# Moving the last shared products and the second half's slot table into the first steps of a loop over sorted expert tiles

## The reference

```python
E = 8; TOP_K = 2; D = 256; DE = 176; DS = 352
shared = jax.nn.silu(x @ Ws_gate) * (x @ Ws_up) @ Ws_down
scores = jax.nn.softmax(x @ W_router, axis=-1)
topk_vals, topk_idx = jax.lax.top_k(scores, TOP_K)
onehot = jax.nn.one_hot(topk_idx, E, dtype=x.dtype)
combine = jnp.einsum('bsk,bske->bse', topk_vals, onehot)
...
h = jax.nn.silu(jnp.einsum('td,edh->eth', xf, We_gate)) * jnp.einsum('td,edh->eth', xf, We_up)
y_all = jnp.einsum('eth,ehd->etd', h, We_down)
routed = jnp.einsum('etd,te->td', y_all, combine)
return routed.reshape(b, s, d) + shared
```

## Time and profile before

| | us |
|---|---|
| median of 3 runs | 673.24 |
| lowest and highest | 670.88, 677.87 |
| the profiled execution | 682.33 |
| its span | 680.6 |

### The profile page before, as it was taken

The page is one execution under the profiler, slowest core; times in us unless marked ns, Lnnn a source line. Parts: engine busy times, 40 slices in busy tenths (PEclk is TensorE's granted clock), DMA queues, the critical chain, the costliest instruction groups (busy, mean ns, idle before and its releaser), DMA issues. The chain is left out here.

```text
span 680.6 us, 16745 instructions
## 1 busy us (share of the span) xinstructions
PE 604.4 (89%) x5027; PEld 460.5 (68%) x5027; DVE 490.6 (72%) x991; ACT 403.7 (59%) x829; POOL 320.1 (47%) x442
## 2 busy tenths in 40 slices
PE   3688877999999968899999999999896799989995
PEld 2577766788888866555555555554674698988874
DVE  2878886688887877889989989983675444444755
ACT  3888883344434431789889889989542154544331
POOL 2455555133232557746656666552675044034163
PEclk9999997999999977799999999999799699999997
DMA  5434448300000024444434444430013145455243
GB/s 162 117 99 133 117 119 298 125 1 1 0 0 1 23 71 141 122 117 152 135 116 145 136 119 143 137 106 6 1 40 110 52 155 171 126 163 172 84 148 116
DMA packets 72601, 71.20 MB, mean 105 GB/s; under 512 B 12364, under 2 KB 68812, under 8 KB 72556
## 3 DMA queue, kind: packets, MB, share of 16 engines
q1 hardware_dynamic: 67324, 56.33, 27.7%
q0 software_dynamic: 5232, 14.29, 6.7%
HBM read 38.48 MB, written 31.36 MB: 103 GB/s over the span
## 5 line engine op out<-in xcount | busy, mean ns | idle before, releaser
L1441 DVE TENSOR_REDUCE a_smax<-a_s 128x2 f32<-128x512 f32 x256 | 165.3, 682 | 16.5 <-PE a_s L1363 11.4
L1259 ACT ACTIVATE a_prob<-a_st 128x512 f32<-128x512 f32 x256 | 141.9, 597 | 20.8 <-PE a_st L1353 19.8
L1353 PEld LDWEIGHTS a_st<-qop,kop 64*128 64x128 f32 x512 | 71.6, 189 | 60.1 <-DVE a_smax L1441 27.9
L1363 PE MATMUL a_s<-kop,qop 64*128 64x256 f32 x512 | 108.8, 323 | 0.0
L1353 PE MATMUL a_st<-qop,kop 64*128 64x256 f32 x512 | 105.2, 317 | 3.4 <-DVE a_smax L1441 2.6
L1315 PE MATMUL last_banks<-a_prob,a_vt 128*32 128x256 f32 x1024 | 82.0, 393 | 3.2 <-ACT a_pv_sb L1244 1.5
L832 POOL TENSOR_TENSOR f_hs_lo<-f_kept,f_hs_hi 128x512 fp32r<-128x512 f32 x32 | 41.3, 1321 | 85.3 <-ACT f_hs_hi L782 85.3
L1363 PEld LDWEIGHTS a_s<-kop,qop 64*128 64x128 f32 x512 | 75.1, 196 | 0.0
L1892 POOL DMA_INDIRECT sorted_rows<-m_xn,m_slot x32 | 32.4, 1014 | 45.0 <-PE m_gu L128 27.4
L126 PE MATMUL f_bank<-f_xt_hi,w_hi 128*128 128x512 f32 x128 | 51.1, 399 | 1.2 <-DVE w_raw L878 0.6
L128 PE MATMUL f_bank<-f_xt_hi,w_lo 128*128 128x512 f32 x128 | 50.3, 393 | 0.0
(11 more groups left out here) (296 smaller groups left out, 1682.3 us busy)
## 6 DMA issues: line engine op xcount, KB each, us to landing
qop<-qop_rows SPq DMA_DIRECT2D x64, 100.0 KB
kop<-kop_rows SPq DMA_DIRECT2D x64, 96.0 KB
sorted_rows<-x_all SPq DMA_DIRECT2D x2, 2944.0 KB, 15.4
qop<-sorted_rows SPq DMA_DIRECT2D x46, 128.0 KB
expert_rows<-turned SPq DMA_DIRECT2D x46, 128.0 KB
kop_rows<-k_hi SPq DMA_DIRECT2D x32, 128.0 KB
qop_rows<-q_hi POOLq DMA_DIRECT2D x30, 128.0 KB, 2.7
x_all<-in_x SPq DMA_DIRECT2D x4, 512.0 KB, 3.8
```

Source lines behind the costliest of these rows:

```text
L1259: act.activation(prob[:, u % 8], st_ps[BANK[u]][:], ACT.Exp, scale=SCALE1).then_inc(prob_ready, 1)
L1353: st = pe.matmul(st_ps[BANK[u]][:, c * D:(c + 1) * D], lhsT=kop[t.slot][rows, u // 2, c * P:(c + 1) * P], rhs=qop[t.slot][rows, u // 2], s ...
L1363: sm = pe.matmul(s_ps[BANK[u]][:, c * D:(c + 1) * D], lhsT=qop[v.slot][rows, w // 2, c * P:(c + 1) * P], rhs=kop[v.slot][rows, w // 2], st ...
L1441: dve.tensor_reduce(smax[:, v.slot, opposite(u)], s_ps[BANK[u]][:].rearrange("p (q n) -> p q n", q=2), AX_X, ALU.max).then_inc(smax_ready, 1)
```

## The change

Four moves, and two waits that follow them. `shared_down(4)` leaves its place ahead of the loop and stands in step 0, behind `turn(0)`; `shared_down(5)` stands in step 2, behind `turn(2)`. `slots(1)` is cut in two: its first seven steps, now `placed(1)`, stay where they were, the rest with `table(1)` goes into step 0 of VectorE's loop, behind the low part of pair 0. `residual(1)` and the scaling of `mix` go into its step 2, behind the low part of pair 2. The expert numbers of the first half now wait for the first 12 table steps only and those from pair 11 on for all 24; `hidden(1)` waits for 19 steps, where it waited for the slots of both halves.

```diff
--- before.py
+++ after.py
@@ -1552,6 +1552,7 @@
         N = GROUPS * SHC
         CHAIN = 17
         TABLE = 12
+        PLACED = 7
         LOGITS = TILES * E
         PLACES = (PT + 1) * E
         LAST_FIRST = (PART_TILES - 1) // 2
@@ -1614,7 +1615,7 @@
                 else:
                     pe.wait_ge(plain_ready, (g - 1) * DC)
                 if g == 2:
-                    pe.wait_ge(table_steps, 7)
+                    pe.wait_ge(table_steps, PLACED)
                 route(pe, misc, second.plain if g == 1 else plain, wr, g).then_inc(logit_done, 1)
 
             def places(b):
@@ -1682,13 +1683,12 @@
                     router(3)
                 if n == 4:
                     places(1)
-            shared_down(HEAD - 2)
-            shared_down(HEAD - 1)
-
             expert_of = {}
 
             def load_experts(p):
                 if p == 0:
+                    pe.wait_ge(table_steps, TABLE)
+                if p == LAST_FIRST:
                     pe.wait_ge(table_steps, TABLE * PARTS)
                 for j in range(2):
                     expert_of[2 * p + j] = pe.value_load(experts_t[0:1, 2 * p + j:2 * p + j + 1], min_val=0, max_val=E - 1)
@@ -1713,7 +1713,7 @@
                     pe.wait_ge(silu_ready, HEAD)
                 else:
                     pe.wait_ge(hid_ready, HEAD)
-                    pe.wait_ge(slot_ready, PARTS)
+                    pe.wait_ge(table_steps, TABLE + PLACED)
                 for j in range(2):
                     e = expert_of[2 * p + j]
                     for dc in range(DC):
@@ -1761,6 +1761,10 @@
                     hidden(s - 2)
                 if s < PAIRS1:
                     turn(s)
+                if s == 0:
+                    shared_down(HEAD - 2)
+                if s == 2:
+                    shared_down(HEAD - 1)
                 if s == PAIRS1 + 2:
                     shared_hidden(HEAD)
                 if s >= 3:
@@ -1992,8 +1996,7 @@
                 op.then_inc(table_steps, 1)
                 dve.wait_ge(table_steps, b * TABLE + k)
 
-            def slots(b):
-                sl = tiles_in(b)
+            def placed(b):
                 counted = misc[:, place_cols(b)]
                 dve.wait_ge(place_done, b + 1)
                 if b == 0:
@@ -2007,6 +2010,9 @@
                 entry(b, 6, dve.tensor_tensor(begins[:], ends[:], tiles_of[:], ALU.subtract))
                 entry(b, 7, dve.scalar_tensor_tensor(place[:], over_tiles(begins[:]), float(P),
                                                      counted[:, 0:PT * E].rearrange("p (t e) -> p t e", e=E), ALU.mult, ALU.add))
+
+            def slots(b):
+                sl = tiles_in(b)
                 for k in range(TOP):
                     op = dve.tensor_tensor(picked[:, k], chosen[:, k, sl], place[:], ALU.mult)
                 entry(b, 8, op)
@@ -2030,6 +2036,7 @@
             choices(0)
             turned_low(1)
             multiply(0)
+            placed(0)
             slots(0)
             table(0)
             for n in range(1, HEAD):
@@ -2044,12 +2051,8 @@
                 if n == 4:
                     residual(0)
                 if n == 5:
-                    slots(1)
-                    table(1)
+                    placed(1)
             hidden_low(HEAD - 1)
-            residual(1)
-            dve.tensor_tensor(mix[:].rearrange("p k t -> p (k t)"), mix[:].rearrange("p k t -> p (k t)"),
-                              gates[:, 3:4].to_broadcast([P, TOP * TILES]), ALU.mult).then_inc(mix_ready, 1)
 
             dve.wait_ge(h_clear, 1)
             for s in range(PAIRS1 + 3):
@@ -2070,6 +2073,13 @@
                     dve.wait_ge(xthi_ready, s + 1)
                     dve.tensor_tensor(xt[1][:, s % 2], xt_ps[:].rearrange("p (c n) -> p c n", c=2),
                                       raw(xt[0][:, s % 2]), ALU.subtract).then_inc(xt_ready, 1)
+                if s == 0:
+                    slots(1)
+                    table(1)
+                if s == 2:
+                    residual(1)
+                    dve.tensor_tensor(mix[:].rearrange("p k t -> p (k t)"), mix[:].rearrange("p k t -> p (k t)"),
+                                      gates[:, 3:4].to_broadcast([P, TOP * TILES]), ALU.mult).then_inc(mix_ready, 1)
                 if s == PAIRS1 - 1:
                     dve.wait_ge(mix_ready, 1)
                     dve.wait_ge(shared_added, PT)
```

## The result

| | before | after |
|---|---|---|
| median, us | 676.38 | 673.76 |
| lowest and highest | 670.88, 684.63 | 667.17, 677.23 |
| runs | 20 | 20 |
| the profiled execution | 682.33 | 667.17 |
| its span | 680.6 | 665.4 |

The ratio of after to before is 0.9942, 95% interval 0.9921 to 0.9963: 0.6% faster, some 3.9 us of 676.4. Forecast were 668.2 us in the range of 664.0 to 673.5; the median of 673.76 lies 0.26 us above that range.

A forecast was written before the change was run, and what follows sets the result against it. TensorE bounds the loop, so the gain is how much earlier its first `turn_hidden` comes: 5.0 us with the clock falling in both kernels. 673.24 - 5.0 = 668.2 us, range 664.0 to 673.5.

The forecast's parts named there:

- The base: Whole kernel: the median of 673.24 us, from which the 5.0 us gain was subtracted to give 668.2.
- the 5.0 of the sum: Way into the loop: first `turn_hidden` 5.0 us earlier, with the clock falling to half in both kernels.
- What the change wins is therefore how much earlier the join comes: Whole kernel: gain equals how much earlier the join (first `turn_hidden`, 544.63 us before) comes, plus what the clock does.
- The steps on VectorE and TensorE: Way into the loop: reordered work leaves the path, so hidden(0) begins at 532.9 instead of 539.47, 6.6 us earlier.
- The idle 0.8 us forecast ahead of turn(1): TensorE ahead of turn(1): one idle time of about 0.8 us, where 2.35 and 1.76 stood.
- The clock: TensorE ahead of the loop: half clock until about 538.7 in the new kernel, covering hidden(0), turn(2) and most of down(5).
- rival 1: Way into the loop: clock stays up in the new kernel only, 7.9 us and 0.3 more, 665.0 us; chance 0.25.
- Rival 2: Ahead of the loop: turn(0) waits for its data, down(4) behind it; gain 0 to 2 us, 672.2; chance 0.20.
- the sign that I named as proof against the prediction: TensorE at turn(0): an idle time ended by a load would show the prediction wrong.
- Rival 3: Way into the loop: late pair 0 data decides turn(1) in both kernels; costs 0.6 to 2.6 us, to 675.8; chance 0.10.
- Rival 4: First three loop steps: residual(1) ahead of `m_gxt_lo` loses 1.66 us in each, giving the gain back, 673; chance 0.05.
- the slack of 1.1 us: First loop step: `m_gxt_lo`, 1.9 us behind the first `turn_hidden`, is ahead of down(0)'s need at 3 us.

The follow-up runs named there:

- after_half_c: The kernel after with only each token's first choice scattered in the first half, on a chip without stretches: 660.48 us, ratio 0.9858 to the kernel before.
- again: The kernel after, unchanged, run once more on a chip without stretches: 666.86 us, ratio 0.9986 to the kernel before.
- before_look: The kernel before, unchanged, run once for its trace on a chip without stretches: 665.56 us.
- before_half_b: The kernel before with only each token's first choice scattered in the first half, on a chip with stretches: 672.24 us, ratio 0.9900 to the kernel before.
- after_half: The kernel after with only each token's first choice scattered in the first half, on a chip with stretches: 669.65 us (4 runs), ratio 0.9830 to the kernel before.

## Why the prediction was wrong, point by point

**The base.** The step that put the time out of the range is "I carry the difference over: 673.24 - 5.0 = 668.2". That median of three runs was 3.1 us below the median of twenty, 676.38, with the runs from 670.9 to 684.6. With the same 5.0 us and the base of 676.38 the time would have been 671.4. As a ratio the forecast was 668.2 / 673.24 = 0.9925, against 0.9942 (0.9921 to 0.9963) in the first comparison and 0.9926 on the other chip with stretches. The class, under 1% faster, held. A forecast given as a ratio would have held too: 0.9925 lies in the interval. That the gain of 3.9 us lies so near the 5.0 of the sum is in part luck. The join moved by 2.5 us more than I had, and over 3 us of it did not reach the time. So a second step failed, though it did not decide the range: "What the change wins is therefore how much earlier the join comes". The next step took 0.2 us of it back (0.7 where the old kernel has full clock in it), and some 3 us more are unexplained.

**The steps on VectorE and TensorE** held in the trace of the first comparison. Turn(0) begins at the end of down(3) with no wait for a load (523.73); hidden(0) follows turn(1) by 1.49 us, where I had 1.75; down(5) fills the wait for `m_h`; slots and table cost nothing beside turn(1). The idle 0.8 us forecast ahead of turn(1) is absent, since down(4) filled it at half clock. Down(3)'s start to hidden(0) was to take 6.07 us (526.83 to 532.9) and took 6.41.

**The clock** was mis-sized. I took the half clock for hidden(0), turn(2) and down(5), 6.7 us from hidden(0) to the join; it took 3.88, at full clock. It fell ahead of that, during down(3), turn(0) and down(4), where it costs little, since at full clock turn(1) waits for the low part of pair 0 instead: down(3) to turn(1) took 4.92 us, and 4.70 in after_half_c at full clock, with 1.31 of them idle. I had 4.32. (The rule that I drew from the Trainium skill, "TensorE: Matmul & The Clock Gate", section "A second HAM failure mode: psum-queue depth-cycling", had the fall stay in both kernels. It stayed in after and is absent from 519 to 528 in after_half_c.) The term at the join was 5.0 and measured 7.5, nearer to rival 1 (7.9), and yet rival 1's time did not come: 7.5 at the join gave 3.9 in the time.

**Rival 2** was the missing condition. In the one trace taken in the first comparison it did not occur, so its 0.20 is not shown wrong there; the mistake was to treat it as chance within one chip. I worked it out from the three stretches of the earlier trace rows for a "median run" of the same chip. It goes with the chip, or with the time at which it was used, which can't be told apart here since each was used once: three of them show no such stretch in any trace, run the kernel before in 666.6 to 668.9 us, and give the change 0.1 to 0.3%. In again down(3) ends near 521.6, turn(0) stands until 527.20, and against before_look the join moves by 1.0 to 1.2 us; I had 522, 527 and 0.3 (0 to 2). There the sign that I named as proof against the prediction, a turn(0) whose idle time is ended by a load, stands in the trace. The 20 runs of the first comparison look like those of a chip with stretches: both profiled traces have them, and the runs spread as widely as on the other (672.7 to 686.2).

**Rival 3** did not occur; where landings are traced, pair 0 lands 2.6 us behind its load, not with the last of the eight. **Rival 4**, as a loss of 1.66 us in each of three steps, did not either, but a loss of 0.7 us in one step did, and it comes from the slack of 1.1 us that I had behind `m_gxt_lo`. I set its start, 1.9 us behind the join, against down(0) at 3 us. It started at 1.95 us, but it takes 0.68 us, and the last transpose of turn(3) began 2.7 us behind the join. Down(0) followed the end of `m_gxt_lo` by 0.14 us: the slack was gone.

## What to carry to other kernels

Work moved out of a wait pays only if the wait's other end does not have its own date: write down when the data lands beside when the engine would be ready, and treat their order as the condition of the whole sum. Here that order differed from chip to chip, so one trace gave the right mechanism and a gain that three of the five later chips don't show (on them it was 0.1 to 0.3%, with an interval clear of zero on one only). Take a base from the median of many runs or give a ratio; three runs out of a spread of 14 us moved mine by 3 us.

## What was not expected of the hardware

ScalarE and VectorE stood still for up to 8.4 us at a time, with nothing of the program as releaser, while or just after GpSimd issued its 16 indirect scatters: 8.21 us on ScalarE until 520.81 and 4.90 on VectorE until 520.01 in the kernel after, with the last scatter issued at 517.98. Traces of two chips and those of the first comparison show it; traces of three others, of the same programs, show none. In before_half_b, on one of the chips that show it, 8 scatters in place of 16 gave no such stretch ahead of 530 us, and the three other such traces on these chips show one only, 1.18 us on VectorE in after_half. From the first scatter to the start of down(3) it is 23.6 to 25.1 us with the stretches, 18.6 without (the kernels before and after), and 19.1 to 20.0 with half the scatters on the same chips. So the stretches hang on the scatters and on the chip or the time of its use; what they are, the traces don't tell.

Most scatters are issued 1.27 us apart (516.71, 517.98), and the load follows the first by 22.6 to 23.8 us in 16 transfers and by 12.4 to 13.0 in 8, with and without stretches alike.
